# A chain of four convolution layers over eight images: the last image's iteration written by itself

## The chip, the cores and the metric

The kernel runs on one core of one Trainium2 chip. A core has five engines with queues of their own: TensorE (PE, matrix products into the eight PSUM banks), VectorE (DVE), ScalarE (ACT), GpSimd (POOL) and SyncE (SP), which here issues all DMAs. They meet only in semaphores. The metric is the device time of one execution in microseconds (us). All data are float32; most matrix products take their operands as float32 split into a high and a low part.

## What is computed

Eight images of 64 x 64 pixels with 48 channels go through four layers one after another.

```python
x = L0(x)   # attention over the tokens of an image, then convolutions 1x1, 3x3, 1x1 on [attn, x], plus x
x = L1(x)   # relu, depthwise 3x3, pointwise 48 -> 48, batch norm
x = L2(x)   # mixture of experts, see below
x = L3(x)   # as L1, with weights of its own

# L2
pooled = jnp.mean(x, axis=(1, 2))
rw = sigmoid(pooled @ Wr + br)                      # 4 experts, one set of weights for each image
h = relu(bn(x @ einsum('be,ecm->bcm', rw, Wpw) + (rw @ bpw)))        # 48 -> 192 channels, "expansion"
h = relu(bn(sum_e depthwise3x3(h, Wdw[e]) * rw[e]))                  # "taps"
h = bn(h @ einsum('be,emf->bmf', rw, Wpwl) + (rw @ bpwl))            # 192 -> 48, "projection"
return h + x
```

The weights of L2 depend on the mean of the whole image after L1. So the expansions of an image can't start before its L1 is through, its mean taken, and the weights mixed.

## The kernel before

An image is held with channels on partitions: two rows of pixels (even, odd) stand in two halves of the partitions, so a chunk of 512 columns is 16 image rows and there are `PCHUNKS` = 4 chunks in an image. The 3x3 layers L1 and L3 are 15 matmuls per chunk (`pair_conv`); they read the tile itself (`a_parts`) and copies of it, shifted by a row or so, that six DMAs per chunk make (`copy_beside`, lines 895 and 899). Those copies of L1 and L3 share one place, `b_parts`.

The 192 channels of L2 lie in `h1a` (128 channels, whole image) and `h1b` (64 channels, the image in two halves on the partitions). The depthwise 3x3 is nine taps: each reads a shifted view and adds into `dwa` or `dwb`. A unit is 16 rows: units 0 and 1 are `dwb`, units 2 to 5 are `dwa`. A step is one tap of one unit, 1024 elements per partition, on DVE (line 669). Units go in pairs that alternate, so that a step never follows the one that it depends on. ACT does the first tap of units 2 to 5 (`first_tap`) and the relu at the end (`finish_unit`, line 1429).

The program is a software pipeline over images. `iteration(f, attn, back)` exists on each engine with an order of its own, written out by hand. It holds, for image f, conv2 and the last product of L0, L1, the router, the weights and the expansions; for image `attn` = f + 1 the attention and conv1; for image `back` = f - 1 the taps that remain, the projection, L3 and the output. Images 1 to 6 run in a loop. The last call has `attn` = None, `back` = 6; after it, image 7 still has its taps, projection, L3 and output. In this tail, PE does the taps of units 2 and 3 (`PE_UNITS`, four chunks of 512 columns) as matmuls with diagonal matrices (`last_taps`, line 1238; `tap_diag` lies in `tok`), DVE units 0, 1, 4 and 5.

PE's order in the last call is: conv2; L1 chunk 0; `w3`; projection of image 6, chunks 0 and 1; L1 chunks 1 and 2; projection chunk 2; L1 chunk 3; projection chunk 3; `routing`; L3 of image 6 with its transposes (`out_tokens`); `expand_halo` and the twelve `expand`. A projection chunk starts with two matmuls that bring in the residual from `x2` (`pick`, lines 1258 and 1259), then eight with the mixed weights (line 1262). `x2` of the next image is copied in two halves on SP (`copy_x2`, line 927), each of which waits for the projections of the image before that read the same rows; SP keeps this order: L1's copies, L3's copies for chunk 0, first half of x2, L3's other copies, second half of x2, `store`.

The outputs of L3 are collected in `outc`, which is a part of `dwa`, transposed by PE, and written by ACT to `ot`, which is a part of `dwb`; four DMAs (line 935) bring that to DRAM. The first step of image 7's taps overwrites `dwb`, so DVE waits for this store (`stored`). The mixed biases and taps are in `dyn`, which both the router of image f and the affine pass (`project_affine`, lines 1468 and 1469) of image f - 1 use. Low parts, which DVE makes for L1, x2 and L3 (`l1_low_part`, `x2_low_part`, `l3_low_part`, line 746 and 759), take 512 elements per partition.

Banks: `ring_b` (2, 3) serves L1, the router and the expansions, `ring_c` (4, 5) conv1 and conv2, `ring_d` (6, 7) projection, L3 and transposes.

Of the kernel before, what the change touches and what calls it, by code (L numbers as in the profile page):

```python
# [7 lines left out]
ALU = mybir.AluOpType  # L8
ACT = mybir.ActivationFunctionType
# [14 lines left out]
TAPS = 9  # L24
# [97 lines left out]
def conv_chain_kernel(nc, a, out):  # L122

    ctx = ExitStack()
    with ctx:
# [144 lines left out]
        tap_step = sem("tap_step")  # L270
# [170 lines left out]
        def _(dve):  # L441
# [210 lines left out]
            def depthwise(image, s0, s1, skipped=0):  # L652

                for s in range(s0, s1):
# [7 lines left out]
                    if n >= 2 and t == 1:  # L662
                        dve.wait_ge(tap1_ready, (UNITS - 2) * image + n - 1 - (len(PE_UNITS) if skipped else 0))
# [3 lines left out]
                    else:  # L667
                        dve.wait_ge(tap_step, TAP_STEPS * image + s - 1 - skipped)
                        nc.vector.scalar_tensor_tensor(out=dst, in0=tap_input(n, t), scalar=weight,  # L669
                                                       in1=dst, op0=ALU.mult, op1=ALU.add).then_inc(tap_step, 1)  # L670

            def halo_out(f):
# [3 lines left out]
                for n, (half, r) in enumerate(((slice(0, M2), PAIRS + 1), (slice(M2, M1), 0))):  # L676
                    nc.vector.tensor_scalar(h1b[half, r, 1:W + 1], bank[half, n * W:(n + 1) * W],
                                            dyn[half, Y_B1 + 1:Y_B1 + 2], 0.0, ALU.add, ALU.max).then_inc(h1b_ready, 1)

            def h1b_rows(f, n):  # L680
# [6 lines left out]
                                        dyn[:, Y_B1 + 1:Y_B1 + 2], 0.0, ALU.add, ALU.max).then_inc(h1b_ready, 1)  # L687
# [92 lines left out]
            def mix_weights(f):  # L780
# [3 lines left out]
                weight_chain(nc.vector.tensor_reduce(dyn[:, :], prod[:, :, :], axis=AX.X, op=ALU.add))  # L784
                weight_chain(nc.vector.tensor_tensor(dyn[:, :], dyn[:, :], lin_const[:, :], ALU.add))
# [6 lines left out]
                weight_chain.end()  # L792
                project_weight_chain.begin(dve, f)
                mix(project_weight_chain, pk[:, :, :].rearrange("p c f -> p (c f)"),
                    wpl[:, :, :, :].rearrange("p e c f -> p e (c f)"))
                project_weight_chain.end()
                nc.vector.tensor_copy(pc[:, 0, :], pk[:, 0, :]).then_inc(pc_ready, 1)
# [4 lines left out]
            def iteration(f, attn, back):  # L802
# [14 lines left out]
                if attn is not None:  # L817
                    norms_begin(attn)
# [9 lines left out]
                if attn is not None:  # L828
                    norms_of_q(attn)
                    sums_apart(attn)  # L830
                    norms_end(attn)
                    sums_out(attn)
                halo_out(f)
                if attn is not None:
                    norm_of_k(attn)
# [774 lines left out]
```

## Time and profile before

| | |
|---|---|
| device time, median of 3 runs | 1115.97 us (1115.47 to 1117.39) |
| device time of the profiled run | 1118.24 us |
| its span, first to last instruction | 1116.4 us |
| mean granted clock of TensorE | 0.980 of full |
| busy over the span | PE 93%, DVE 78%, ACT 42%, POOL 8% |
| chain that ended last, over the span | PE 66%, DVE 16%, issue 7%, SPq 4%, DMA 3%, ACT 3% |

The span runs from the first to the last instruction. Shares over the span are means over stages with different limits: the last 140 us, from the end of the last conv2, are some 12% of it. What ends there is read from the timelines of each engine, where a bracket gives the idle time ahead of a row and what released it. SPq is SP's queue of DMA issues. "Issue" in the chain is time in which an engine waited for nothing that the profile shows.

### The profile page before, as it was taken

What the parts mean: (1) busy time and instruction counts of PE and PEld (TensorE: products, weight loads), DVE (VectorE), ACT (ScalarE), POOL (GpSimd) and SP (SyncE); (2) the same over time, 40 slices, a digit from 0 to 9 for tenths busy, and PEclk for the clock granted to TensorE, in tenths of its full rate; (3) what the DMA queues carried; (4) which work ended last, traced back from release to release, by engine and by line L of the source; (5) the groups of instructions that cost most, each with busy time, mean ns of one, the idle gap of its engine ahead of it and who ended that gap; (6) DMA issues with size and microseconds to landing.
All of it is one profiled execution on the core that took longest, in us unless ns stands there. A gap on an engine that the chain in (4) does not pass through costs nothing.

```text
span 1116.4 us, 14998 instructions
## 1 busy us (share of the span) xinstructions
PE 1035.4 (93%) x4808; PEld 658.5 (59%) x4808; DVE 867.4 (78%) x1193; ACT 468.9 (42%) x812; POOL 92.6 (8%) x72
## 2 busy tenths in 40 slices
PE   4699879999999999999999999999999999979986
PEld 3366566666665675666665676666665676636424
DVE  6742579996799959996899959996899959973960
ACT  3311534264623644264623653264623653344321
POOL 0300111001300111001300111001300111000000
PEclk9899979999999999999999999999999999989998
DMA  5226315145433545145423545145423541245014
GB/s 69 53 49 90 79 39 92 30 101 124 95 35 76 108 106 91 30 101 120 97 32 78 110 104 89 34 102 116 102 30 78 111 102 44 40 104 119 19 34 92
DMA packets 124336, 87.19 MB, mean 78 GB/s; under 512 B 96815, under 2 KB 97684, under 8 KB 124308
## 3 DMA queue, kind: packets, MB, share of 16 engines
q1 hardware_dynamic: 124308, 86.83, 39.6%
q8 instruction: 15, 0.25, 0.1%
q14 instruction: 13, 0.11, 0.0%
HBM read 10.82 MB, written 6.29 MB: 15 GB/s over the span
## 4 chain that ended last, share of the span: by engine, by line
PE 66%; DVE 16%; issue 7%; SPq 4%; DMA 3%; ACT 3%; POOL 0%; ACTq 0%; DVEq 0%; POOLq 0%
PE bank L1160 13%; PE bank L1165 12%; PE bank L1171 8%; PE bank L1194 7%; DVE dwa L669 4%; PE bank L1141 4%; PE bank L1262 3%; PE bank L1182 3%; DMA y_parts<-a_parts 3%; DVE a_parts L746 2%; DVE s L592 2%; PE bank L1209 2%; PE bank L1210 2%; PE bank L1197 2%; PE bank L1196 2%
## 5 line engine op out<-in xcount | busy, mean ns | idle before, releaser
L669 DVE SCALAR_TENSOR_TENSOR dwa<-h1a,dyn,dwa 128x1024 f32<-128x1024 f32 x240 | 293.2, 1277 | 0.0
L669 DVE SCALAR_TENSOR_TENSOR dwb<-h1b,dyn,dwb 128x1024 f32<-128x1024 f32 x128 | 155.9, 1276 | 0.0
L1160 PE MATMUL bank<-y_parts,w_l 96*96 96x512 f32 x576 | 151.2, 407 | 0.0
L1165 PE MATMUL bank<-y_parts,w_h 128*96 128x512 f32 x576 | 147.5, 400 | 0.0
L1194 PE MATMUL bank<-a_parts,wt_h 128*112 128x512 f32 x384 | 117.7, 415 | 14.4 <-DMA y_parts<-a_parts 10.8
L1160 PEld LDWEIGHTS bank<-y_parts,w_l 96*96 96x96 f32 x576 | 91.5, 163 | 60.6 <-issue 21.4
L1165 PEld LDWEIGHTS bank<-y_parts,w_h 128*96 128x96 f32 x576 | 93.5, 162 | 44.2
L1194 PEld LDWEIGHTS bank<-a_parts,wt_h 128*112 128x112 f32 x384 | 63.6, 176 | 49.6 <-issue 22.6
L1029 POOL TENSOR_TENSOR y_parts<-y,y_parts 96x512 fp32r<-96x512 f32 x56 | 67.1, 1200 | 246.0 <-DVE y L707 245.9
L1441 ACT ACTIVATE y<-bank,b2s 96x512 f32<-96x512 f32 x32 | 21.9, 683 | 141.1 <-PE bank L1171 141.1
L1171 PE MATMUL bank<-y_parts,w_one 128*96 128x512 f32 x192 | 77.1, 402 | 0.0
L1171 PE MATMUL bank<-y_parts,w_two 128*96 128x512 f32 x192 | 76.7, 399 | 0.0
L1023 POOL TENSOR_TENSOR tok<-tok,u 128x1536 f32<-128x1536 f32 x8 | 24.6, 3072 | 586.5 <-DVE u L594 586.5
L746 DVE SCALAR_TENSOR_TENSOR a_parts<-v,a_parts 112x512 fp32r<-112x512 f32 x64 | 59.0, 932 | 16.7 <-ACT a_parts L1469 13.8
L1441 ACT ACTIVATE xq<-bank,b2s 96x512 f32<-96x512 f32 x32 | 21.9, 685 | 116.0 <-PE bank L1171 107.4
L1141 PE MATMUL bank<-xq,w_cur 97*96 97x512 f32 x128 | 66.8, 603 | 3.4 <-DVE y L707 3.4
L1491 ACT ACTIVATE dwa<-bank,conv_bias,inv 112x512 f32<-112x512 f32 x32 | 24.9, 778 | 102.7 <-PE bank L1197 102.7
L706 DVE TENSOR_TENSOR y_parts<-bank,y 96x512 fp32r<-96x512 f32 x64 | 44.0, 687 | 23.2 <-ACT y L1413 23.1
L1194 PE MATMUL bank<-a_parts,wt_l 128*112 128x512 f32 x192 | 56.7, 404 | 0.0
L1094 PE MATMUL bank<-qkw,xcm 113*128 113x192 f32 x256 | 49.9, 339 | 1.7 <-ACT xcm L1373 1.7
L1197 PE MATMUL bank<-y_parts,wt_h 128*112 128x512 f32 x128 | 51.6, 403 | 0.0
L1196 PE MATMUL bank<-y_parts,wt_h 128*112 128x512 f32 x128 | 51.3, 401 | 0.0
(246 smaller groups left out, 1671.1 us busy)
## 6 DMA issues: line engine op xcount, KB each, us to landing
y_parts<-a_parts SPq DMA_DIRECT2D x64, 198.0 KB, 3.0
y_parts<-a_parts SPq DMA_DIRECT2D x64, 197.6 KB, 3.4
tok<-in_x_dram SPq DMA_DIRECT2D x48, 192.0 KB, 4.9
a_parts<-a_parts SPq DMA_DIRECT2D x128, 66.0 KB, 2.4
y_parts<-y_parts SPq DMA_DIRECT2D x64, 131.9 KB, 2.3
x_even<-y_parts SPq DMA_DIRECT2D x32, 198.0 KB, 3.6
x_odd<-y_parts SPq DMA_DIRECT2D x32, 198.0 KB, 4.0
out_dram<-dwb SPq DMA_DIRECT2D x32, 192.0 KB, 3.6
```

Of the source, the lines that this page charges most:

```text
L669: nc.vector.scalar_tensor_tensor(out=dst, in0=tap_input(n, t), scalar=weight, in1=dst, op0=ALU.mult, op1=ALU.add).then_inc(tap_step, 1)
L706: nc.vector.tensor_tensor(y1_view(y1_h, k - 1), bank.rearrange("p (j w) -> p j w", w=W), y1_tokens(k - 1), ALU.max).then_inc(y1h_ready, 1)
L746: return nc.vector.scalar_tensor_tensor(out=lo[:, rows, 1:W + 1], in0=src[:, m % 2, :].rearrange("p (j w) -> p j w", w=W), scalar=0.0, in1 ...
L1029: nc.gpsimd.tensor_tensor(y1_view(y1_l, k), y1_tokens(k), y1_view(y1_h, k).bitcast(F32), ALU.subtract).then_inc(y1l_ready, 1)
L1094: last = nc.tensor.matmul(bank[:, m * 2 * C2:(m + 1) * 2 * C2], xcm[:, i * 128:(i + 1) * 128], qkw[:, :], start=True, stop=True)
L1141: nc.tensor.matmul(bank[0:C2, :], w1_cur[:, :], xq[:, (k - 1) % 2, :], start=True, stop=True)\
L1160: nc.tensor.matmul(bank[0:C2, :], w2_l[:, t, :], y1_h[:, rows, cols], start=t == 0, stop=False)
L1165: nc.tensor.matmul(bank[0:C2, :], w2_h[:, t, :], y1_parts[:, 0, rows, cols], start=False, stop=False)
L1171: last = nc.tensor.matmul(bank[0:C2, :], wgt[:, kh, :], y1_parts[:, 1, rows, cols], start=False, stop=kh == 2 and kw == 2)
L1194: nc.tensor.matmul(bank[0:P2, :], wgt[layer][:, kw, :], own[:, rows, kw:kw + W], start=n + kw == 0, stop=False)
L1196: nc.tensor.matmul(bank[0:P2, :], wgt[layer][:, 3, :], beside[:, rows, 1:W + 1], start=False, stop=False)
L1197: last = nc.tensor.matmul(bank[0:P2, :], wgt[layer][:, 4, :], beside[:, rows, 2:W + 2], start=False, stop=n == 2)
```

## The change

Iterations 0 to 6 and the tail's functions keep their text but for names. The last call of `iteration` becomes `last_iteration(LAST, LAST - 1)` on PE, DVE, ACT and SP:

- PE does L1 chunks 1, 2 and 3 in one go, then the `pick` matmuls of projection chunks 2 and 3 of image 6 into banks 4 and 5, then `routing`, L3 chunk 0 of image 6, the rest of projection chunks 2 and 3, the expansions, and only then L3 chunks 1 to 3 of image 6 with all transposes. `last_taps`, the projection and L3 of image 7 follow.
- DVE spreads the last eight taps of image 6 between low parts, mean and router; `mix_weights` is cut in `mix_weights`, `mix_project` and `project_weights`, the last of which waits for all projections of image 6.
- ACT does `route` ahead of `finish_unit` of units 4 and 5 of image 6; the nine diagonals follow the expansions.
- SP does both halves of `copy_x2` behind L3's copies for chunk 0; the second half waits for `x2_read`, the new semaphore of the early `pick` matmuls, in place of the projections.
- For image 6, `outc` is in `xcm` and `ot` in `tok`; for image 7, `dyn` is in `tok`. DVE no longer waits for a store.
- PE does the taps of chunks 0, 1 and 7 (three, before four); DVE units 0 and 1, then 3 and 4, then unit 5 with 8 rows in place of 16. Its eight steps follow each other alone, and `l3_low_part(f, 0)` stands ahead of the last four.
- The final store is cut in two: three quarters, then the last quarter, four DMAs each.

The diff, cut to the new orders and the places:

```diff
+        def last_unit(n):
+            src, dst, c, r0 = unit(n)
+            rows = ROWS if n == UNITS - 1 else UNIT_ROWS
+            taps = [src[:, r0 + t // 3:r0 + t // 3 + rows, t % 3:t % 3 + W] for t in range(TAPS)]
+            return taps, dst[:, 0:rows, :], c
...
+        LAST_STEPS = ([(n, t) for t in range(TAPS) for n in (0, 1)] + [(n, t) for t in range(1, TAPS) for n in (3, 4)]
+                      + [(5, t) for t in range(1, TAPS)])
...
-        PE_UNITS = (2, 3)
-        PE_CHUNKS = len(PE_UNITS) * UNIT_ROWS * W // BANK
-        PE_BANKS = (0, 1, 4, 5)
-        tap_diag = tok[:, :, :, :].rearrange("p b i c -> p (b i c)")[:, 0:TAPS * 128]
...
+        PE_CHUNKS, PE_BANKS = (0, 1, 7), (0, 1, 4)
+        PROJECT_BANKS = {2: 4, 3: 5}
+        LAST_FINISHED = {0: 4, 1: 6, 2: 7, 3: 8}
+        tok_flat = tok[:, :, :, :].rearrange("p b i c -> p (b i c)")
+        tap_diag = tok_flat[:, 0:TAPS * 128]
+        dyn_last = tok_flat[:, TAPS * 128:TAPS * 128 + Y_ALL]
+        ot_apart = tok_flat[:, RUN * TOK:RUN * TOK + 2 * RUN * C]
+        def dyn_of(image):
+            return dyn_last if image is LAST else dyn[:, :]
+        def outc_of(image):
+            return xcm[0:P2, :] if image is LAST - 1 else outc
+        def ot_of(image):
+            return ot_apart if image is LAST - 1 else ot
...
+            def last_iteration(f, back):
+                conv2_out(f, back)
+                depthwise_at(back, BY_PROJECT)
+                w3_out(f, PCHUNKS - 1)
+                depthwise_at(back, BY_PROJECT + 1)
+                l1_low_part(f, PCHUNKS - 1)
+                depthwise_at(back, BY_PROJECT + 2)
+                x2_low_part(f, 0)
+                l3_low_part(back, 0)
+                l3_low_part(back, 1)
+                depthwise_at(back, BY_PROJECT + 3, steps=slice(0, 1))
+                x2_low_part(f, 1)
+                depthwise_at(back, BY_PROJECT + 3, steps=slice(1, 3))
+                x2_low_part(f, 2)
+                depthwise_at(back, BY_PROJECT + 3, steps=slice(3, 5))
+                mean_out(f)
+                x2_low_part(f, 3)
+                depthwise_at(back, BY_PROJECT + 3, steps=slice(5, 7))
+                route(f)
+                depthwise_at(back, BY_PROJECT + 3, steps=slice(7, None))
+                mix_weights(f)
+                mix_project(f)
+                l3_low_part(back, 2)
+                dve.wait_ge(project_done, 2 * PCHUNKS * f)
+                project_weights()
+                halo_out(f)
+                l3_low_part(back, 3)
+                for n in range(4):
+                    h1b_rows(f, n)
+                dve.wait_ge(h1b_ready, H1B_WRITES * (f + 1))
+                before_last = len(LAST_STEPS) - (TAPS - 1) // 2
+                depthwise_last(slice(0, before_last))
+                l3_low_part(f, 0)
+                depthwise_last(slice(before_last, None))
+                for m in range(1, PCHUNKS):
+                    l3_low_part(f, m)
...
+            if f is LAST and half == 1:
+                wait(sp, x2_read, PCHUNKS // 2)
...
+            beside_l1(sp, LAST)
+            beside_l3(sp, LAST - 1, IMAGES, (0,))
+            copy_x2(sp, LAST, 0)
+            copy_x2(sp, LAST, 1)
+            beside_l3(sp, LAST - 1, IMAGES, range(1, PCHUNKS))
+            store(sp, LAST - 1)
+            beside_l3(sp, LAST, IMAGES)
+            store(sp, LAST, range(3))
+            store(sp, LAST, range(3, 4))
+            sp.wait_ge(stored, 16 * STORES * (IMAGES + 1))
...
+            def out_and_l3(image):
                 for m in range(2, PCHUNKS):
                     out_tokens(image, (m - 2,))
                     l3(image, (m,))
-                out_tokens(image, (PCHUNKS - 2,))
+                out_tokens(image, (PCHUNKS - 2, PCHUNKS - 1))
...
+            def last_iteration(f, back):
+                conv2(f)
+                l1(f, (0,))
+                w3(f, PCHUNKS - 1)
+                project(back, (0, 1))
+                l1(f, (1, 2, 3))
+                for m in (2, 3):
+                    project_x2(banks[PROJECT_BANKS[m]], m).then_inc(x2_read, 1)
+                routing(f)
+                l3(back, (0,))
+                project(back, (2, 3), begun=True)
+                expand_halo(f)
+                for n in range(12):
+                    expand(f, n)
+                l3(back, (1,))
+                out_and_l3(back)
+                last_taps(f)
+                project(f, range(PCHUNKS))
+                l3(f, (0, 1))
+                out_and_l3(f)
...
+            def last_finish(n):
+                _, dst, _ = last_unit(n)
+                act.wait_ge(tap_step, last_value(n, TAPS - 1))
+                nc.scalar.activation(dst, dst, ACT.Relu).then_inc(h2_ready, 1)
+            def taps_out(nth):
+                n, b = PE_CHUNKS[nth], PE_BANKS[nth]
+                act.wait_ge(taps_done, nth + 1)
+                nc.scalar.activation(dwa[:, n * ROWS:(n + 1) * ROWS, :], banks[b][:, :].rearrange("p (j w) -> p j w", w=W),
+                                     ACT.Relu, bias=dyn_last[:, Y_DWB:Y_DWB + 1]).then_inc(h2_ready, 1)
...
+            def last_iteration(f, back):
+                conv2_slope(f, back)
+                l1_high_part(f, PCHUNKS - 1)
+                l1_out(f, (0,))
+                project_affine(back, f + 1, 0)
+                project_affine(back, f + 1, 1)
+                l1_out(f, (1, 2, 3))
+                route(f)
+                finish_unit(back, 4)
+                finish_unit(back, 5)
+                project_affine(back, f + 1, 2)
+                project_affine(back, f + 1, 3)
+                l3_out(back, (0,))
+                act.wait_ge(weight_chain.sem, weight_chain.each * (f + 1))
+                for n in range(4, 12):
+                    h1a_rows(f, n)
+                for t in range(TAPS):
                     nc.scalar.activation(tap_diag[:, t * 128:(t + 1) * 128], ident[:, :], ACT.Copy,
-                                         scale=dyn[:, Y_DW + t:Y_DW + t + 1]).then_inc(diag_ready, 1)
-                conv1_slope(attn, f)
+                                         scale=dyn_last[:, Y_DW + t:Y_DW + t + 1]).then_inc(diag_ready, 1)
+                act.wait_ge(h1a_ready, H1A_WRITES * (f + 1))
+                l3_out(back, (1,))
+                last_first_tap(3)
+                tokens_out(back, (0,))
+                last_first_tap(4)
+                l3_and_tokens_out(back, (2,))
+                last_first_tap(5)
+                l3_and_tokens_out(back, (3,))
+                tokens_out(back, (PCHUNKS - 1,))
+                last_finish(0)
+                last_finish(1)
+                for nth in range(len(PE_CHUNKS)):
+                    taps_out(nth)
+                project_affine(f, IMAGES, 0)
+                last_finish(3)
+                last_finish(4)
+                project_affine(f, IMAGES, 1)
+                last_finish(5)
+                project_affine(f, IMAGES, 2)
+                project_affine(f, IMAGES, 3)
+                l3_out(f, (0,))
+                l3_and_tokens_out(f, range(1, PCHUNKS))
+                tokens_out(f, (PCHUNKS - 1,))
```

`last_first_tap` is as `first_tap`, with the units above; `mean_out`, `route`, `halo_out`, `h1b_rows`, `conv2_out`, `conv2` and `conv2_slope` are unchanged.

## Rows read from the trace of the kernel before

**Rows 1.** The chain that ended last, 975 to 1117 us: start us, us, what.
```profile
1032.48 3.97 DMA out_dram<-dwb
```

**Rows 2.** Timeline of PE, 975 to 1117: start, us, operation, count [idle before, releaser].
```profile
989.24 0.94 PE L1194 MATMUL bank<-a_parts,wt_h 128*112 128x512 f32 x3 [0.70 <-DMA y_parts<-a_parts]
...
999.19 0.74 PE L1258 MATMUL bank<-x_odd,pick 96*112 96x512 f32 x1 [6.17 <-ACT dwa L1429]
...
1028.94 0.48 PE L1209 MATMUL bank<-x_even,ew_h 96*128 96x512 f32 x1
...
1038.95 0.40 PE L1210 MATMUL bank<-x_odd,ew_l 96*128 96x512 f32 x1
1039.19 31.07 PE L1238 MATMUL bank<-h1a,tok 128*128 128x512 f32 x72
1069.69 0.81 PE L1258 MATMUL bank<-x_odd,pick 96*112 96x512 f32 x1
...
1072.53 0.49 PE L1258 MATMUL bank<-x_odd,pick 96*112 96x512 f32 x1
...
1078.58 0.49 PE L1258 MATMUL bank<-x_odd,pick 96*112 96x512 f32 x1 [3.48 <-ACT a_parts L1469]
...
1082.78 0.49 PE L1258 MATMUL bank<-x_odd,pick 96*112 96x512 f32 x1
...
1087.29 0.94 PE L1194 MATMUL bank<-a_parts,wt_h 128*112 128x512 f32 x3 [1.91 <-DMA y_parts<-a_parts]
...
1092.85 1.48 PE L1194 MATMUL bank<-a_parts,wt_h 128*112 128x512 f32 x3 [1.76 <-DMA y_parts<-a_parts]
...
1099.02 0.96 PE L1194 MATMUL bank<-a_parts,wt_h 128*112 128x512 f32 x3 [0.48 <-ACT dwa L1491]
...
1103.70 0.97 PE L1194 MATMUL bank<-a_parts,wt_h 128*112 128x512 f32 x3 [0.48 <-ACT dwa L1491]
```

**Rows 3.** Timeline of DVE, same stretch and columns.
```profile
988.29 1.29 DVE L746 SCALAR_TENSOR_TENSOR a_parts<-v,a_parts 112x512 fp32r<-112x512 f32 x2
989.50 9.65 DVE L669 SCALAR_TENSOR_TENSOR dwa<-h1a,dyn,dwa 128x1024 f32<-128x1024 f32 x8
...
1013.08 0.26 DVE L783 TENSOR_TENSOR mixed<-lin,rw 128x92 f32<-128x92 f32 x1 [0.75 <-ACT rw L1486]
...
1018.09 0.39 DVE L799 TENSOR_SCALAR pc<-mixed,mask_half 128x48 f32<-128x48 f32 x2
...
1033.21 0.75 DVE L685 TENSOR_SCALAR h1b<-bank,dyn 128x512 f32<-128x512 f32 x1 [0.22 <-PE bank L1210]
1036.48 1.53 DVE L665 TENSOR_SCALAR dwb<-h1b,dyn 128x1024 f32<-128x1024 f32 x2 [2.52 <-DMA out_dram<-dwb]
...
1057.06 19.22 DVE L669 SCALAR_TENSOR_TENSOR dwa<-h1a,dyn,dwa 128x1024 f32<-128x1024 f32 x16
...
1079.79 0.69 DVE L746 SCALAR_TENSOR_TENSOR a_parts<-v,a_parts 112x512 fp32r<-112x512 f32 x1 [0.46 <-ACT a_parts L1469]
```

**Rows 4.** Timeline of ACT, same stretch and columns.
```profile
1011.54 1.28 ACT L1486 ACT_TABLE_LOAD   x1
...
1029.60 2.73 ACT L1558 ACTIVATE tok<-ident,dyn 128x128 f32<-128x128 f32 x9
...
1075.12 2.25 ACT L1429 ACTIVATE dwa<-dwa 128x1024 f32<-128x1024 f32 x2 [4.14 <-DVE dwa L669]
```

**Rows 5.** Timeline of SP's queue, same stretch: start, us, DMA issues.
```profile
982.57 1.22 SPq L895 DMA_DIRECT2D a_parts<-a_parts  x2
...
986.79 1.24 SPq L895 DMA_DIRECT2D a_parts<-a_parts  x2
...
1080.58 1.34 SPq L895 DMA_DIRECT2D a_parts<-a_parts  x2
...
1109.67 3.42 SPq L935 DMA_DIRECT2D out_dram<-dwb  x4
```

**Rows 6.** Windows: busy time of each engine, then granted clock, DMA share, GB/s.
```profile
1079.00:1083.00 4.00, 4.00 (x11) 0.86 (x10) 1.02 (x2) 0.76 (x3) 0.00 (x0) 0.57 0.19 30
```

More of the change, by code:

```diff
@@ L650, in depthwise_at, with depthwise @@
                     depthwise(image, chosen.start, chosen.stop)
-            def depthwise(image, s0, s1, skipped=0):
+            def depthwise(image, s0, s1):
                 for s in range(s0, s1):
@@ L858, in _ @@
                 iteration(f, f + 1, f - 1)
-            iteration(IMAGES - 1, None, IMAGES - 2)
-            for m in range(PCHUNKS):
-                l3_low_part(IMAGES - 1, m)
+            last_iteration(LAST, LAST - 1)
         def wait(sp, semaphore, value):
@@ L927, in copy_x2, with store @@
                     sp.dma_start(dst, src).then_inc(x2_copied, 16)
-        def store(sp, image):
-            wait(sp, ot_ready, 4 * image + 4)
+        def store(sp, image, chunks=range(4)):
+            wait(sp, ot_ready, 4 * image + chunks.stop)
             dst = out[image].rearrange("(i j b) w c -> j b w i c", j=STEP, b=2)
+            runs = slice(chunks.start * RUN // 4, chunks.stop * RUN // 4)
             for j in range(STEP):
-                src = ot[j * W:(j + 1) * W, :].rearrange("p (b i c) -> p b i c", b=2, c=C)
+                src = ot_of(image)[j * W:(j + 1) * W, :].rearrange("p (b i c) -> p b i c", b=2, c=C)
                 for par in range(2):
-                    sp.dma_start(dst[j, par], src[:, par]).then_inc(stored, 16)
+                    sp.dma_start(dst[j, par][:, runs, :], src[:, par, runs, :]).then_inc(stored, 16)
         def beside_l1(sp, f):
@@ L1187, in pair_conv @@
                 for m in chunks:
-                    bank = ring.take(pe, image, places[m])
+                    if layer == L3 and image is LAST - 1 and m == 0:
+                        pe.wait_ge(ah3_ready, PCHUNKS * image + 1)
+                        bank = ring.bank(places[m])
+                    else:
+                        bank = ring.take(pe, image, places[m])
                     pe.wait_ge(b_copied[layer][m], 16 * B_COPIES * (image + 1))
@@ L1232, in last_taps @@
                 pe.wait_ge(diag_ready, TAPS)
[L1233 to L1235 removed]
+                pe.wait_ge(h1a_ready, H1A_WRITES * (image + 1))
+                for n, b in zip(PE_CHUNKS, PE_BANKS):
                     for t in range(TAPS):
@@ L1256, in project @@
                     other = dwb[:, :, :].rearrange("p (j b) w -> p j b w", b=2)[:, m2 * ROWS:(m2 + 1) * ROWS]
-                    rows = slice(m * ROWS, (m + 1) * ROWS)
-                    nc.tensor.matmul(bank[0:P2, :], pick[:, :], x2[1][:, rows, 1:W + 1], start=True, stop=False)
-                    nc.tensor.matmul(bank[0:C, :], pick[:, ODD_AT:P2], x2[0][:, rows, 1:W + 1], start=False, stop=False)
+                    if not begun:
+                        project_x2(bank, m)
                     for n, (part, src) in enumerate(((0, first), (1 + m // 2, other))):
@@ L1272, in out_tokens @@
                         i = 4 * n + m
-                        last = nc.tensor.transpose(bank[:, m * P2:(m + 1) * P2], outc[:, i * 128:(i + 1) * 128], ident[0:P2, 0:P2])
+                        last = nc.tensor.transpose(bank[:, m * P2:(m + 1) * P2], outc_of(image)[:, i * 128:(i + 1) * 128], ident[0:P2, 0:P2])
                     last.then_inc(outt_done, 1)
```

127 lines of the change are left out of this document (59 added, 68 removed).

## The prediction

> **What bounds the kernel now.** I read the chain of waits for the last 140 us first [rows 1], then the timelines of PE, DVE, ACT and of SP's queue in the same stretch [rows 2 to 5], then the clock by windows [rows 6]; everything ahead of the last image's conv2 is untouched by the change, and its loop is the same code. The stretch to read begins at 988.29 us, where VectorE (DVE) still works off image 6's depthwise taps. Four things are to be seen.
>
> First, the front. After image 6's last eight taps (9.65 us) come the router of image 7, its weights (1013.08 us) and then 10 us in which DVE has nothing, since TensorE (PE) works through layer 3 of image 6 ahead of the expansions; these begin at 1028.94 us [rows 2, 3]. PE itself had stood still for 6.17 us before 999.19 us, because the projection of image 6 waits for DVE's taps and stands ahead of L1's chunk 3 [rows 2].
>
> Second, DVE's run. Image 7's own taps begin at 1036.48 us, 2.52 us late: `ot`, the output of image 6, lies in `dwb`, and its store (3.97 us in the chain) must have read it [rows 1, 3]. From there DVE works without a gap: 20.58 us to the row at 1057.06 us, then 19.22 us [rows 3]. PE's four chunks of taps, 1039.19 to 1069.69 us, lie beside this and end earlier; PE then waits 3.48 us for DVE and ScalarE (ACT) before 1078.58 us [rows 2]. So DVE bounds this stage.
>
> Third, the end. From the first copy for layer 3 of image 7 (1080.58 us) to the end of the span are 35.8 us of copies, four chunks, transposes, store [rows 2, 5].
>
> Fourth, the clock. Over 1079 to 1083 us the granted clock averages 0.57 of full, so nearly all of it is the level of 1.2 GHz instead of 2.4 [rows 6]; the projection of a chunk takes 4.20 us there (1078.58 to 1082.78) against 2.84 (1069.69 to 1072.53) [rows 2].
>
> **The change part by part.** All times are moments of the profiled execution, as they would be after the change; its span is 1116.4 us.
>
> *The router chain.* L1's chunks 2 and 3 now follow each other on PE. A set of six copies is usable 6.67 us after its first issue (982.57 to 989.24 us); chunk 3's set is issued at 986.79 us, so it is usable at 993.5 us, against a chunk that ran after the 6.17 us wait [rows 2, 5]. A chunk of L1 or layer 3 is 15 matmuls and takes 3.8 us: 4.68 between the starts at 1099.02 and 1103.70, less 0.48 idle and some 0.4 for transposes [rows 2]. PE is through at 997.3. DVE has from 988.29 us, in order, six low parts of 0.60 us (two take 1.21, the next row's start less this row's), seven of the eight remaining taps at 1.20 (eight take 9.65, the last not overlapped), the mean and the router's add at 0.8 and short waits for ACT of together 0.8 (my estimates, from L1 chunks ending at 993.0 and 997.3) [rows 2, 3]. Sum 13.6: router input ready at 1001.9. The sigmoid's table load (1.28 us) and the sigmoid with its hand-overs (some 0.4) give 1003.55 [rows 4]. The weights take from 1013.08 to about 1018.0 us before, 4.9 us with the mix for the projection: 1008.45 [rows 3].
>
> Moved behind the sigmoid are ACT's two finishing passes over image 6 (2.25 us, [rows 4]): they end at 1005.8. Projection chunks 2 and 3 wait on PE for them, and PE can begin at 1004.75, in place of 999.19. Their two `pick` matmuls each are done earlier, into banks 4 and 5 that conv2 has left, so that the second copy of x2 need only await those. About 1.9 us a chunk remains (2.84 less some 0.95, an estimate): done at 1008.5. So weights and projection arrive together, and neither hides the other by more than 0.1 us. The x2 copies are not in the way: their second half is issued from about 999.6, and even at 6.67 us it is there at 1006.3. Layer 3's chunk 0 runs ahead of this in PE's wait, from 999.1 to 1002.9 (its copies, issued at about 991, are usable at 997.7).
>
> *The expansions.* They start at 1009.0 in place of 1028.94, a gain of 19.9 us. The twelve take 10.4 us (to 1039.35) [rows 2]; I add 0.4 because a low part of image 6 and the projection's weights stand between them on DVE: done at 1019.8. DVE's four h1b passes end 5.0 us after the expansions' start (1033.21 + 0.75) [rows 2, 3]; here 5.3: DVE is free for image 7's taps at 1014.35, without the wait for a store, since `ot` of image 6 now lies in `tok`: 22.1 us earlier.
>
> *What now lies ahead of PE's taps.* Layer 3's chunks 1 to 3 of image 6. A chunk follows the one before it by 4.68 us (1099.02 to 1103.70), as ACT empties the bank between [rows 2]. 1019.8 + 2 x 4.68 + 3.8 for the last + 1.4 for its emptying and transposes = 1034.4: PE's taps begin there, against 1039.19. Their copies are on SP from 1009.2, three sets 4.22 us apart, so all are usable by 1024.4 and hidden. ACT's nine diagonals (2.73 us, [rows 4]) lie beside layer 3's chunk 1, at no cost; if that cover went they would cost 2.7.
>
> *The units split anew.* PE does three chunks of taps and not four. One is 30.50 / 4 = 7.62 us [rows 2]: taps end at 1034.4 + 22.9 = 1057.3. DVE gets eight half-size steps more. Unlike the others they run alone, each waiting for the one before it. Full steps go at 1.20; a low part with 512 elements is 0.69 [rows 3], so a step is between 0.60 and 0.75, taken as 0.72. DVE: 1014.35 + 20.58 + 19.15 = 1054.1, then four half steps, 1057.0. Thus the bound passes from DVE to PE. DVE has about 4 us of slack.
>
> *From taps to copies.* The first projection runs from 1057.3 to 1060.2 (2.84). Before the second, ACT must do the affine pass (1.2: from 1075.12 + 2.25 = 1077.37 to PE's 1078.58) and unit 3's finish (1.1), which stands behind it in ACT's queue though its data were ready at 1053 [rows 2, 4]: 1062.65. Second projection 2.84, affine 1.25, DVE's low part 0.7: copies of layer 3 are issued at 1067.55, against 1080.58 [rows 3, 5], so 13.0 us earlier. On DVE, `l3_low_part(f, 0)` waits until 1061.4 with four half steps queued behind it; they end at 1065.1 and the next low part needs DVE only at 1066.8.
>
> *The end.* Sets 4.22 us apart, each usable after 6.7: chunk 0 at 1074.25, chunk 1 at 1078.5, chunk 2 at 1083.2, chunk 3 at 1087.9. From chunk 3's start to the end are 12.7 us now (1103.70 to 1116.4) [rows 2]: 1100.6. The store is cut into two of four DMAs. Four issues take 3.42 us [rows 5]; the first group begins some 0.9 earlier than the one store, the second is issued behind it. Bounds: 0.9 us less (if transfer, not issue, ends last) to 2.5 more (the second group's issue added and nothing saved); I take +0.3, near the lower end, since the second group moves a quarter of the data. Sum at full clock: 1100.9.
>
> On this split the Trainium skill, "DMA: Bandwidth & Descriptors", section "Anatomy of one DMA", gives each DMA a fixed cost of about 2.0 us whatever its size. By that the small last DMAs would be through 2 us after their issue and the end would come 0.3 us before that of an uncut store, so the sum would be 0.6 lower; no run here shows a small DMA to DRAM.
>
> *The clock.* PE's idle times after the change are 1.95 us (1002.9 to 1004.8), 2.4 us (1060.2 to 1062.65) and 3.4 us (1070.9, when the last projections are through, to 1074.25). Now, 6.17 and 3.48 us idle are followed by low clock (after the first, a `pick` matmul takes 0.74 against 0.49), and the idle of 1.76 us before 1092.85 too: three matmuls take 1.48 there against 0.96 at 1099.02 [rows 2]. I charge the two longer ones: 1.4 us for a projection (4.20 less 2.84) or up to 1.7 with what follows, taken as 1.7, and 1.3 for layer 3, where chunk 0 has 0.5 us of slack and the spell before 1099.02 cost 1.5 (6.17 from 1092.85, less 4.68). Sum 1103.9. The shortest may cost 0 to 1.7 and is left at 0.
>
> **Against the median.** The span of the profiled run, 1116.4, stands 0.43 above the median of 1115.97. 1103.9 - 0.4 = 1103.5 us, 1.1% less than before.
>
> **The rivals.**
> *Full clock (chance 0.15).* The idles pass without the low level, as the 1.91 us before 1087.29 did [rows 2]: 1100.5 us.
> *More waits (0.22).* The short idle costs its 1.7 too, the split store 1 and the hand-overs that I took at their best 1: about 1107 us. For it: every hand-over between engines in my sum is a best case.
> *DVE stays the bound (0.05).* Its work grows to 45.6 us. With its start at D, layer 3's copies follow at D + 46.2; that passes PE's 1067.55 from D = 1021.4 on, 7 us later than worked out. At D = 1028: about 1109 us.
> *The expansions stay late (0.03), slower.* The mechanism is PE's order: 14.6 us of image 6's layer 3 now stand between expansions and taps. Copies follow the expansions' end E by 47.75 us. If E stayed at 1039.35, because the router or the x2 copies came no earlier, they would be issued at 1087.1 and the end would be at some 1123 us. It decides against the change from E = 1034 on; I have 1019.8. Against it speaks that each of its inputs is there by 1008.5.
> *It does not act (0.02).* Both effects cancel near E = 1032: 1116 us.
>
> **How the numbers follow.** The forecast itself (1101.5 to 1106) has 0.53. The range 1099.5 to 1109 takes in the first three cases and half of the fourth; some 0.1 is left out. Some 0.2% (2.2 us) is what a measurement of this kernel can tell from no change. The first four cases are faster (0.95), the last is no change (0.02), the fifth slower (0.03).
>
> **What the profile would show.** Right: routing on PE near 999 and the sigmoid near 1003; the first expansion near 1009; DVE's first tap of image 7 near 1014; PE's taps from 1034 to 1057, in three chunks; DVE idle before `l3_low_part(f, 0)`; layer 3's copies at 1067 to 1070; the last store DMA issued behind a first group. Wrong: expansions after 1012, PE's taps beginning after 1037, or DVE with no gap before the last image's low parts.

## The result and the profile after

The changed kernel takes 1106.95 us (median of 4 runs, 1106.4 to 1108.68) against 1116.68 us for the kernel before on the same chip (4 runs): a ratio of 0.9901, interval 0.9876 to 0.9926. The same kernel again on another chip, in six runs, gave 0.9921 (0.9895 to 0.9948). 1103.5 us was forecast, 1.1% less; it is 1.0% less.

The profiled execution has a span of 1106.9 us. Its page, first and second part (busy us and share of the span; then clock in 40 slices):

```profile
PE 1030.5 (93%) x4790; PEld 658.3 (59%) x4790; DVE 872.8 (79%) x1201; ACT 469.6 (42%) x813; POOL 92.6 (8%) x72
PEclk9799969999999999999999999999999999998998
```

The shares hardly differ from those before; what changed is in the last 125 us. The engines' timelines after (start us, us, operation, count [idle before, releaser]), PE first:

```profile
1001.11 0.36 PE L1294 MATMUL bank<-wr,routed 112*128 112x4 f32 x2 [0.60 <-DVE routed L809]
...
1009.58 0.48 PE L1300 MATMUL bank<-x_even,ew_h 96*128 96x512 f32 x1
...
1011.98 0.51 PE L1300 MATMUL bank<-x_odd,ew_h 96*128 96x512 f32 x1 [1.21 <-DVE h1b L720]
...
1013.49 0.80 PE L1300 MATMUL bank<-x_even,ew_h 96*128 96x512 f32 x1 [0.22 <-DVE h1b L728]
...
1024.73 0.63 PE L1301 MATMUL bank<-x_odd,ew_l 96*128 96x512 f32 x1
...
1040.33 23.36 PE L1328 MATMUL bank<-h1a,tok 128*128 128x512 f32 x54
1063.12 0.81 PE L1334 MATMUL bank<-x_odd,pick 96*112 96x512 f32 x1
...
1068.35 0.49 PE L1334 MATMUL bank<-x_odd,pick 96*112 96x512 f32 x1 [2.33 <-ACT dwa L1538]
...
1080.03 0.94 PE L1285 MATMUL bank<-a_parts,wt_h 128*112 128x512 f32 x3 [4.07 <-DMA y_parts<-a_parts]
...
1094.44 0.97 PE L1285 MATMUL bank<-a_parts,wt_h 128*112 128x512 f32 x3 [0.48 <-ACT dwa L1612]
```

DVE, ACT and SP's queue:

```profile
984.15 6.06 DVE L696 SCALAR_TENSOR_TENSOR dwa<-h1a,dyn,dwa 128x1024 f32<-128x1024 f32 x5
...
1005.41 0.25 DVE L826 TENSOR_TENSOR mixed<-lin,rw 128x92 f32<-128x92 f32 x1
...
1018.10 1.53 DVE L707 TENSOR_SCALAR dwb<-h1b,tok 128x1024 f32<-128x1024 f32 x2
1019.55 19.22 DVE L712 SCALAR_TENSOR_TENSOR dwb<-h1b,tok,dwb 128x1024 f32<-128x1024 f32 x16
1038.68 22.25 DVE L712 SCALAR_TENSOR_TENSOR dwa<-h1a,tok,dwa 128x1024 f32<-128x1024 f32 x20
1067.46 0.69 DVE L789 SCALAR_TENSOR_TENSOR a_parts<-v,a_parts 112x512 fp32r<-112x512 f32 x1 [6.54 <-ACT a_parts L1590]
1068.07 3.11 DVE L712 SCALAR_TENSOR_TENSOR dwa<-h1a,tok,dwa 128x512 f32<-128x512 f32 x4
```

```profile
1001.13 1.28 ACT L1607 ACT_TABLE_LOAD   x1
1004.33 0.20 ACT L1607 ACTIVATE rw<-rwz 128x4 f32<-128x4 f32 x1 [1.92 <-DVE rwz L814]
```

```profile
1073.18 1.31 SPq L972 DMA_DIRECT2D a_parts<-a_parts  x2
...
1099.55 5.49 SPq L1016 DMA_DIRECT2D out_dram<-dwb  x8
```

The bound has passed from DVE to PE: DVE now stands idle for 6.54 us before its first low part of image 7, and PE's taps run until its projection without a gap. Before, DVE waited 2.35 us at that place, for ACT's finish and affine pass, which themselves waited for DVE's last tap:

```profile
1078.64 0.69 DVE L746 SCALAR_TENSOR_TENSOR a_parts<-v,a_parts 112x512 fp32r<-112x512 f32 x1 [2.35 <-ACT a_parts L1469]
```

DVE's taps begin with no wait for a store.

And the surprise, in windows (busy us of PE, PEld, DVE, ACT, POOL; granted clock; DMA share; GB/s): over 1014 to 1026 us PE is busy all the time and at half clock, 1.2 GHz.

```profile
1001.00:1011.00 10.00, 9.27 (x41) 4.85 (x41) 9.33 (x22) 6.62 (x10) 0.00 (x0) 1.00 0.47 107
1014.00:1026.00 12.00, 12.00 (x26) 7.05 (x25) 9.50 (x11) 5.47 (x9) 0.00 (x0) 0.50 0.71 155
1063.00:1076.00 13.00, 10.63 (x42) 2.68 (x40) 5.00 (x7) 6.89 (x10) 0.00 (x0) 1.00 0.08 13
```

**A better ruler.** DVE's row of five taps of image 6 (1024 elements each) ends the part that the change leaves alone. It starts at 982.31 us before and at 984.15 us after, and between 981.3 and 987.1 us in all twelve profiles of this study. The two profiles of one same kernel (e2 and e9 below) have it at 981.32 and 986.07 us, so the scatter is no part of an edit; in these two all of it is there by 170 us. It is as large as most effects here. So profiles are compared by the **stretch** from the start of that row to the end of the span; before it is 1116.4 - 982.31 = 134.1 us (one profile only), after 1106.9 - 984.15 = 122.8 us. The timings, which hold the whole kernel, are given with their intervals.

### The profile page after: what moved, and what is told of

The parts are those of the page before. It is cut to its first block, busy times and chain, and to the rows that moved or that the text cites. A ratio compares the mean times of both kernels' runs of the same rounds, so it can differ in the third digit from the quotient of the medians.

```text
span 1106.9 us, 14973 instructions
## 1 busy us (share of the span) xinstructions
PE 1030.5 (93%) x4790; PEld 658.3 (59%) x4790; DVE 872.8 (79%) x1201; ACT 469.6 (42%) x813; POOL 92.6 (8%) x72
## 4 chain that ended last, share of the span: by engine, by line
PE 70%; DVE 12%; issue 7%; SPq 4%; ACT 3%; DMA 3%; POOL 0%; ACTq 0%; DVEq 0%; POOLq 0%
PE bank L1247 13%; PE bank L1252 12%; PE bank L1258 8%; PE bank L1285 8%; PE bank L1228 5%; PE bank L1300 3%; PE bank L1269 3%; PE bank L1301 3%; DMA y_parts<-a_parts 2%; DVE s L619 2%; DVE a_parts L789 2%; PE bank L1350 2%; PE bank L1288 2%; DVE dwa L696 2%; PE bank L1287 2%
## 5 line engine op out<-in xcount | busy, mean ns | idle before, releaser
L696 DVE SCALAR_TENSOR_TENSOR dwa<-h1a,dyn,dwa 128x1024 f32<-128x1024 f32 x224 | 274.1, 1275 | 0.0
L696 DVE SCALAR_TENSOR_TENSOR dwb<-h1b,dyn,dwb 128x1024 f32<-128x1024 f32 x112 | 136.6, 1275 | 0.0
L1247 PEld LDWEIGHTS bank<-y_parts,w_l 96*96 96x96 f32 x576 | 91.6, 163 | 60.7 <-issue 21.3
L1612 ACT ACTIVATE dwa<-bank,conv_bias,inv 112x512 f32<-112x512 f32 x28 | 21.8, 778 | 91.2 <-PE bank L1288 91.2
```

The lines of the kernel that those rows point to most:

```text
L1247: nc.tensor.matmul(bank[0:C2, :], w2_l[:, t, :], y1_h[:, rows, cols], start=t == 0, stop=False)
```

## The experiments

### The changed kernel again

> The changed kernel itself, unedited, on the chip of the next three, to see how much of its time moves between executions and whether the low clock in the expansions comes back. If the low clock of 13.7 us there belongs to the kernel, the stretch from image 6's five taps (VectorE's row of five steps ahead of the first low part of x2) to the end is again about 122.7 us. If the length of the low spell is chance, this stretch lies between 119.5 and 123 us. The ratio to the kernel before should be 0.988 to 0.993.

Ratio 0.9921 (0.9895 to 0.9948); stretch 122.6 us, against 122.8. The low clock came back at the same place and for 13.7 us, as it did in the profile of the kernel with the whole store below. The stretch is repeatable to some 0.2 us here, and to 0.35 us in the two profiles of the filled kernel below; the times of single executions ranged from 1104.2 to 1112.7 us.

### The idle ahead of the second expansion: moved, or filled

```diff
                 mix_project(f)
+                halo_out(f)
                 l3_low_part(back, 2)
                 dve.wait_ge(project_done, 2 * PCHUNKS * f)
                 project_weights()
-                halo_out(f)
```

> The changed kernel with one line moved: on VectorE halo_out(f) stands straight behind mix_project(f), ahead of the low part of image 6 and of project_weights. In the changed kernel TensorE waits 1.21 us for halo_out ahead of the second expansion and the granted clock falls 1.3 us later, for 13.7 us. Theory A (that idle is what brings the clock down): the idle shrinks to about 0.3 us, the expansions run at the 2.4 GHz level, end some 3.7 us earlier, and the kernel takes 1106.9 - 1.0 - 3.0 = about 1103 us. Rival B (the clock falls for what the projections and small matmuls before it do, whatever the wait): the clock still falls near 1013 us, only the wait is saved, and of its 1 us most is lost to the slower matmuls: 1106 to 1107 us.

Ratio 0.9888 (0.9864 to 0.9913), stretch 120.0 us, no low clock in the expansions. But the idle didn't shrink as expected; it moved to the next expansion:

```profile
1011.50 0.50 PE L1300 MATMUL bank<-x_odd,ew_h 96*128 96x512 f32 x1 [0.21 <-DVE h1b L720]
...
1014.01 0.50 PE L1300 MATMUL bank<-x_even,ew_h 96*128 96x512 f32 x1 [1.30 <-DVE h1b L728]
```

So this run does not speak for theory A by its own argument: an idle of 1.30 us was there and the clock held. In a later kernel with the same line moved (e7) it fell for 3.4 us. And further on the clock fell where it had not in the changed kernel, at the second projection, behind an idle of the same length (2.33 us in both):

```profile
1064.75 0.77 PE L1334 MATMUL bank<-x_odd,pick 96*112 96x512 f32 x1 [2.33 <-ACT dwa L1538]
```

The cleaner test leaves every wait where it is and gives PE work in it:

```diff
                 expand_halo(f)
-                for n in range(12):
+                expand(f, 0)
+                for _ in range(5):
+                    nc.tensor.matmul(banks[0][:, :], ew_h[:, 0:M1], x2[0][:, 0:ROWS, 1:W + 1], start=True, stop=True)
+                for n in range(1, 12):
                     expand(f, n)
```

> The changed kernel with five matmuls of 512 columns more, into bank 0 that nobody reads, between the first and the second expansion, where TensorE now stands idle for 1.21 us. The wait for VectorE stays as it is. Five at 0.24 us are 1.2 us, so nothing is delayed at full clock. Theory A (the idle brings the clock down): full clock through the expansions, about 3 us less, 1103.5 to 1104.5 us. Rival B (not the idle but the work before it): the low clock comes all the same and the five matmuls cost up to 1 us: 1107 to 1108 us.

> The same kernel as e2 (the changed kernel with five idle-filling matmuls behind the first expansion), for a second profile. Without them the low clock came in the expansions in five profiles of five that have this order (13.7 us three times, 3.4 us twice). Theory A (the idle brings it): again no low clock between the first expansion and TensorE's taps, 120.0 to 120.3 us from image 6's five taps to the end. Rival B (it was chance in e2): a spell of 3.4 or 13.7 us, 121 to 123 us.

Ratios 0.9874 (0.9852 to 0.9895) and 0.9888 (0.9868 to 0.9909). Both profiles have no low clock between the first expansion and PE's taps; stretches 120.2 and 120.5 us, the second 0.2 us above what was expected. The first of them, in windows:

```profile
1009.00:1020.00 11.00, 10.03 (x34) 5.64 (x35) 10.08 (x12) 5.80 (x10) 0.00 (x0) 1.00 0.68 141
1020.00:1026.00 6.00, 5.46 (x27) 3.90 (x25) 6.00 (x6) 5.61 (x12) 0.00 (x0) 1.00 0.34 80
```

In five profiles of kernels with this order and nothing in the idle, the clock fell in the expansions five times (13.7 us in the two profiles of the changed kernel and in that with the whole store, 3.4 us in the old split and the two chunks); in three with the idle filled (these two and e8) it did not. From the first expansion's start to the end of the last are 15.8, 13.6 and 12.2 us for a spell of 13.7, of 3.4 and none. This supports theory A, and it puts the price of the long spell at 3.6 us by the end of the expansions. The clean comparison is two filled profiles against five: e8 also has `halo_out` moved, and in that order one of two profiles without filling (e1) held its clock too.

Adding useless work made the kernel's stretch 2.3 us shorter (120.4 against 122.7, means of two profiles each). It is less than the price of the spell, because part is given back: PE's taps begin 4.3 us earlier in the stretch, but in e1, e2 and e9 a low spell now comes at the second projection, which takes 4.1 to 4.2 us (3.7 in e9, and its third is slow too) in place of 2.5. In the timings the gain over the changed kernel (0.990 and 0.992) is within the intervals, so the profiles carry this claim.

### The old split of the units in the new order

```diff
-        PE_CHUNKS, PE_BANKS = (0, 1, 7), (0, 1, 4)
+        PE_CHUNKS, PE_BANKS = (0, 1, 2, 3), (0, 1, 4, 5)
...
-                      + [(5, t) for t in range(1, TAPS)])
+        LAST_STEPS = [(n, t) for t in range(TAPS) for n in (0, 1)] + [(n, t) for t in range(1, TAPS) for n in (4, 5)]
```

> The changed kernel with the units split as in the kernel before: TensorE takes four chunks of taps (units 2 and 3), VectorE units 0, 1, 4 and 5; everything else as changed. Theory (TensorE's row of taps bounds the stage after the change): taps end 7.6 us later, at about 1070.7, layer 3's copies go out near 1078 to 1080, and the kernel takes 1112 to 1114.5 us, so order and places alone are worth only some 3 us of the 10. Rival (VectorE still bounds): its work shrinks by about 3 us, and the kernel takes 1104 to 1107 us.

Ratio 0.9955 (0.9937 to 0.9973), 1115.1 us on a chip where the kernel before took 1119.2; stretch 126.7 us. DVE is through early and waits:

```profile
1040.33 19.21 DVE L711 SCALAR_TENSOR_TENSOR dwa<-h1a,tok,dwa 128x1024 f32<-128x1024 f32 x16
1074.31 0.69 DVE L788 SCALAR_TENSOR_TENSOR a_parts<-v,a_parts 112x512 fp32r<-112x512 f32 x1 [14.77 <-ACT a_parts L1586]
```

That is the theory: order and places alone bring about half, since PE's taps then bound; the new split brings the rest, 0.9955 to 0.990, although it gives DVE, the bound of the kernel before, more work. By the stretch the first part looks larger, 7.4 of 11.4 us, but 2.2 us of that are the shorter low spell in this profile's expansions (3.4 us, not 13.7).

### Two chunks on PE

```diff
-            rows = ROWS if n == UNITS - 1 else UNIT_ROWS
+            rows = UNIT_ROWS
...
-        PE_CHUNKS, PE_BANKS = (0, 1, 7), (0, 1, 4)
+        PE_CHUNKS, PE_BANKS = (0, 1), (0, 1)
```

> The changed kernel with two chunks of taps on TensorE in place of three, and unit 5 whole on VectorE (eight steps of 1024 elements alone, about 1.36 us each, in place of eight of 512), with the low parts for layer 3 placed among them. Theory (TensorE bounds, VectorE has 6.5 us idle before its first low part): taps end at 1055.5, layer 3's first copies go out some 7 us earlier, but the fourth chunk's projection waits for unit 5 until about 1071, which gives back one or two: 1099 to 1102 us. Rival (VectorE becomes the bound at once, as it has no room for 5 us more): 1104 to 1108 us.

Ratio 0.9851 (0.9828 to 0.9875), stretch 116.8 us: six us less than the changed kernel. The first set of copies goes out 82.3 us into the stretch, against 89.0, the second only at 87.9, for a low part behind lone steps. The fourth projection waits 6.27 us for unit 5, as the theory had it, and then runs at low clock (its first `pick` takes 0.74 us).

### The store in one piece

```diff
-            store(sp, LAST, range(3))
-            store(sp, LAST, range(3, 4))
+            store(sp, LAST)
```

> The changed kernel with the last store in one piece: four DMAs behind the last transposes, as before, in place of four for three quarters and four for the rest. In the prediction the split cost 0.3 us, with bounds of 0.9 us less and 2.5 more. Theory A (issue time bounds the end): from the start of the last chunk of layer 3 to the end 12.2 us with the store whole, against 12.46 in the changed kernel's profile. Theory B (transfer bounds it, the early three quarters gain): 12.7 us, as in the kernel before. The rest of the kernel is the same, so the difference of the medians is under 0.5 us and can't be told from the timing, only from that stretch.

From the start of the last chunk of layer 3 to the end: 12.76 us whole, against 12.46 and 12.42 in the two profiles of the changed kernel and 12.70 before. Theory B: cutting the store gains 0.3 us. Issuing ends 3.37 us before the end of the span with the store whole (3.31 before) and 1.86 us before it with the small DMAs last. The timing (0.9923, 0.9897 to 0.9949) can't show it.

### The places alone, on the kernel before

```diff
+        def ot_of(image):
+            return ot_apart if image is NEXT_TO_LAST else ot
...
-                        after(dve, stored, 16 * STORES * image)
+                        if image is not IMAGES - 1:
+                            after(dve, stored, 16 * STORES * image)
```

> The kernel before with one part of the change: outc and ot of image 6 lie in xcm and tok, and VectorE no longer waits for the store of image 6. Nothing else is moved. Theory (VectorE bounds the stage, so its start decides): its run starts 2.5 us earlier, all later steps follow, and the kernel takes 2.5 us less, a ratio of 0.9978. Rival (something else is due just behind): TensorE's taps end at 1069.7 us, before VectorE's 1073.7, so nothing of the 2.5 us is lost to them; if all the same less than 1 us comes, the bound of the prediction's first part was misread.

Ratio 0.9980 (0.9964 to 0.9995), as expected. The profile confirms the mechanism and not the amount: DVE's taps follow its last h1b pass at once,

```profile
1035.89 0.75 DVE L696 TENSOR_SCALAR h1b<-bank,dyn 128x512 f32<-128x512 f32 x1 [0.21 <-PE bank L1221]
1036.68 1.53 DVE L676 TENSOR_SCALAR dwb<-h1b,dyn 128x1024 f32<-128x1024 f32 x2
```

but in this execution the expansions began 2.5 us later in the stretch than before: a set of copies for layer 3 had a slow issue (2.14 us for two, else 1.23), PE idled 1.92 us for it, and low clock followed. DVE's taps therefore start where they did in the stretch (54.2 us), and the stretch is 133.4 against 134.1 us.

### Towards a faster kernel

```diff
+                last_finish(3)
                 project_affine(f, IMAGES, 0)
-                last_finish(3)
                 last_finish(4)
                 project_affine(f, IMAGES, 1)
-                last_finish(5)
                 project_affine(f, IMAGES, 2)
+                last_finish(5)
```

This, with `halo_out` moved, two chunks on PE and the low parts spread among the lone steps, is e7:

> A kernel built from the first experiments: the changed kernel with halo_out ahead of the low part, two chunks of taps on TensorE and unit 5 whole on VectorE, the low parts for layer 3 spread among its lone steps (behind the first, fourth, sixth and eighth), and on ScalarE the finish of unit 3 ahead of the first affine pass, that of unit 5 behind the third. With two chunks alone the stretch from image 6's five taps to the end was 116.8 us, with layer 3's second set of copies 1.4 us late for a low part that stood behind unit 5. Theory (these are separate waits and add up): 1.5 us from halo_out, 1 us from the finish, 1.5 to 2.5 us from the low parts: 111.5 to 113.5 us in that stretch, a ratio to before of 0.980 to 0.983. Rival (TensorE's idle behind two chunks brings the low clock onto the projections and layer 3, which eats it): 114.5 to 116.5 us, 0.983 to 0.986.

Ratio 0.9879 (0.9852 to 0.9907), stretch 117.1 us. That is the rival's mechanism, and 0.6 us beyond its range: the three edits together brought nothing over two chunks alone (116.8 us). The first copies go out at 79.8 us, but the last projection waits for unit 5 and runs at low clock (a `pick` of 0.74 us, as in [rows 2] after the 6.17 us):

```profile
1073.58 0.74 PE L1333 MATMUL bank<-x_odd,pick 96*112 96x512 f32 x1 [8.11 <-ACT dwa L1537]
```

The last kernel puts work into that idle: PE does chunk 7's taps there, and DVE has unit 5 in half size again. It also has three matmuls that nobody reads behind the first expansion, and the low parts for layer 3 placed anew.

```diff
-                last_taps(f)
-                project(f, range(PCHUNKS))
+                last_taps(f, slice(0, 2))
+                project(f, range(3))
+                last_taps(f, slice(2, 3))
+                project(f, (3,))
```

> Built from e7, whose last projection waited 8.11 us on TensorE for unit 5 and then ran at the 1.2 GHz level. Here TensorE does the taps of chunk 7 again (7.7 us), but behind the third projection, in that idle time, and VectorE unit 5 in half size; three idle-filling matmuls stand behind the first expansion, halo_out ahead of the low part, finishes and low parts spread as in e7. Theory (TensorE's idle behind its first two chunks was the cost, and can be filled): full clock from the expansions to the last projection, the last projection at its start about as in e7 but at full speed, low parts done 2 us earlier, the expansions 1.4 us shorter: 113 to 114.5 us from image 6's five taps to the end (e7 117.1, the changed kernel 122.7), a ratio to before of 0.980 to 0.984. Rival (the copies for layer 3 bound and nothing comes of it): 116.5 us or more, 0.986 or more.

1099.54 us (5 runs, 1098.3 to 1102.8) against 1116.69: ratio 0.9847 (0.9823 to 0.9870). Stretch 114.7 us, and the granted clock is full from the expansions to the last chunk.

```profile
1058.62 7.99 PE L1327 MATMUL bank<-h1a,tok 128*128 128x512 f32 x18
1067.49 0.46 PE L1333 MATMUL bank<-x_odd,pick 96*112 96x512 f32 x1 [0.87 <-ACT dwa L1547]
```

The 114.7 us are just above the 113 to 114.5 expected. Of the 2.5 us gained on e7, 1.4 are the expansions (12.1 us, against 13.4 with a low spell there) and the rest lies behind them; no run has the late chunk alone. It is faster than the kernel before and the changed kernel; from the one with two chunks alone (0.9851) the timings don't tell it apart, the stretch does (114.7 against 116.8).

## Why the prediction was right, and where it was off

Moments within the stretch (predicted: the sum's time less 982.31; measured: the profile after, less 984.15):

| step | predicted | measured |
|---|---|---|
| mix of the weights begins | 21.2 | 21.3 |
| first full expansion | 26.7 | 25.4 |
| DVE's taps of image 7 | 32.0 | 34.0 |
| expansions end | 37.5 | 41.2 |
| PE's taps | 52.1 | 56.2 |
| first, second projection | 75.0, 80.3 | 79.0, 84.2 |
| copies for layer 3 issued | 85.2 | 89.0 |
| end, with 3.0 for the clock | 121.6 | 122.8 |

**Right: the mechanism and the passing of the bound.** Router and expansions ahead of layer 3, DVE free of the store, three chunks of taps in 22.8 us (22.9), PE as the bound, DVE with slack, the chain from the first projection to the copies (projection, affine, finish, projection, affine, low part) in 10.1 us (10.25; the terms given for it add up to 9.9, so 0.3 us of that sum had no term). The old split and two chunks show the bound from both sides. The slower rival fell with the expansions' end: they ended at 1025.4 us, some 10 us ahead of where it decides.

**Near in part by luck.** In the stretch the end came 1.2 us later than the sum had it, but the errors behind that are larger: 5.0 us too little for the expansions, against 1.3 for their earlier start, 1.7 charged for low clock at the second projection and not met, and 0.9 too much behind the copies. As a time, 1106.95 us lies outside the forecast itself (1101.5 to 1106), inside the range, and on the number of the rival "More waits" (about 1107). Of the 3.0 us between the sum and the span (1103.9 and 1106.9), 1.84 are the later start-up of the profiled execution. Of that rival's three items the hand-overs did cost (1.21 us in the expansions), the short idle shrank to 0.40 us at full clock, and the cut store gained.

**The step that failed: "The expansions".** They were priced at full clock with 0.4 us added, and took 15.8 us in place of 10.8, though they began 1.3 us earlier than the sum had them: they wait for `mix_weights` alone, not for `mix_project`, and the projection ahead of them on PE was done 1.2 us early as well. Nearly all of the 4 us that PE's taps were late comes from here. The filled kernels show that 3.6 us of it are low clock. Beside it, DVE did `halo_out` behind a low part and the projection's weights, and PE waited 1.21 us for it; the 0.4 us were meant for this, and as a place where the clock can fall the wait was in none of my idles.

**"The clock": the total too low by a third, one place of three right.** 1.7 us were charged to the second projection; it followed 2.33 us of idle at full clock (the window of 1063 to 1076). 1.3 us to layer 3's chunk 0: it took 5.15 us and cost some 1.1 (an estimate: chunk 1 began at 1085.18, and its copies, issued from 1077.41 and usable some 6.7 us later, would have let it begin at 1084.1; the prediction's own rows, 1.5 less 0.5 of slack, give 1.0). The expansions, at nothing, cost 3.6. A charge of 3.0 stood for 4.7. That idle of 1.2 us was followed by low clock and one of 2.33 was not, so the length of one idle doesn't decide it. The same idle of 2.33 to 2.34 us before the second projection was followed by full clock in four profiles (both of the changed kernel, the whole store, the two chunks) and by low clock in three (e1, e2, e9), where it cost some 1.6 us, the size of the charge. So the charge had the right price for a thing that comes in some kernels and executions only.

**"The router chain": two errors that cancelled.** The table load was put on the path with 1.28 us. It ran as soon as ACT was free and was through 1.92 us before the sigmoid could start. But the router's add came behind two taps, 0.5 us late, and the mix behind one more: it began when foreseen.

**"The units split anew": outside my bounds.** A lone half step was put between 0.60 and 0.75 us; four take 3.11 us, 0.78 each. Four lone steps of full size take 5.24 us in the kernel with two chunks, 1.31 each. From the two sizes the part that does not scale is about 0.25 us. The Trainium skill, "VectorE: DVE Perf Modes", section "The TRN2 errata", has such a fixed extra time per instruction, 151 cycles in its formula for an fp32 `tensor_tensor` or 0.16 us. The runs show more for steps that each wait for the one before. Of the eight, none was on the critical path.

**"The end": wrong in sign.** +0.3 us for the cut store was -0.3, by one profile of the whole store. Eight issues took 5.49 us and not 6.8, for the smaller ones go faster. What I had set beside it, the Trainium skill's fixed cost of 2.0 us in "DMA: Bandwidth & Descriptors", section "Anatomy of one DMA", gave the right sign: by it a gain of 0.3 us. The section has that figure for DMAs issued by GpSimd, and these are issued by SyncE. Here the span ended 1.86 us after the issuing of the last small DMA, near that figure, and 3.37 us after that of the last whole one; no more can be said for the 0.3 us, since the prediction gives no working for it.

**"Against the median".** The span was set 0.43 us above the median of the device times. But device time is some 1.8 us above its own span (1108.68 and 1106.9 here, 1118.24 and 1116.4 before): the profiled execution of before was itself 2.3 us slower than the median, and the one after 1.7. The two nearly cancel on both sides, so this did no harm.

**What stays open.** Why the spell lasted 13.7 us in three profiles and 3.4 in two with the same code up to there. By the row of five taps the three began at 982.81 to 985.07 us and the two at 986.19 and 986.41, so the length may go with the moment at which an execution arrives there; no run varies that moment alone. Open too is why the second projection lost its clock in some kernels; and why PE, busy throughout 1014 to 1026 us, did not bring the clock back sooner. No run here tells.

## What to carry to other kernels

When a stage's bound is taken away by an earlier start, size what is then late on every other engine and split the work between them anew, in both directions: here the order alone was worth half of the gain, and PE, not the old bottleneck, had to be relieved. Fill an idle of TensorE that can't be removed with work that is needed anyway (taps of a later chunk), or even with matmuls that nobody reads; here it was worth more than the idle, 2.3 us for 1.2. Compare profiles from an event behind the unchanged part, when the start-up scatters by more than the effect.

## What the runs showed of the hardware that was not expected

An idle of 1.2 us of TensorE was followed by up to 13.7 us at 1.2 GHz although the engine was then busy without a gap (12.00 of 12.00 us), and by none when five matmuls filled it. An idle of 2.33 to 2.34 us at one place was followed by full clock in four profiles and by low clock in three. An activation table load doesn't wait for the input of its activation: it ran from 1001.13 us, its activation's input was made at 1004.15. The start-up of one and the same program moved by 4.75 us between two executions (981.32 and 986.07 us at a fixed instruction), and over all twelve profiles by 5.8 us.
